# A decoder layer's state-space mixer: eight resident Toeplitz tiles, a re-ordered prologue and a token buffer with the chunk index innermost

## The reference

```
x = x + mixer(layernorm(x))       # diagonal state-space scan, projection 256 -> 256, its own residual
x = x + cross_attention(layernorm(x), ctx)     # 16 heads of 16, 64 keys
x = x + ffn(layernorm(x))         # 256 -> 2x1024 gated -> 1024 -> 1024 -> 256

mixer(u):  xn = layernorm(u) * gamma + beta
           h[t] = exp(-exp(log_A) dt) h[t-1] + (B dt) xn[t]       # 64 states per channel
           y[t] = sum_n C[n] h[t][n] + D xn[t]
           return u + y @ W_out.T + b_out
```

## Time and profile before

| | before |
|---|---|
| median of 3 runs | 929.63 us (928.91 to 930.36) |
| the profiled execution, its own time | 931.86 us |
| its span, first to last instruction | 929.9 us |
| PE / PEld busy | 865.2 us (93%) / 703.3 us (76%) |
| DVE / ACT / POOL busy | 524.3 (56%) / 483.3 (52%) / 183.7 us (20%) |
| granted TensorE clock, mean | 0.985 |
| code fetched by PE's queue (q8) | 24 packets, 0.39 MB |

### The profile page before, as it was taken

The page is one execution under the profiler, slowest core; times in us unless marked ns, Lnnn a source line. Parts: engine busy times, 40 slices in busy tenths (PEclk is TensorE's granted clock), DMA queues, the critical chain, the costliest instruction groups (busy, mean ns, idle before and its releaser), DMA issues.

```text
span 929.9 us, 15452 instructions
## 1 busy us (share of the span) xinstructions
PE 865.2 (93%) x5762; PEld 703.3 (76%) x5762; DVE 524.3 (56%) x943; ACT 483.3 (52%) x745; POOL 183.7 (20%) x201
## 2 busy tenths in 40 slices
PE   1168999899999999999999999999999999999998
PEld 0067867677887778777877787778777887788887
DVE  7996486465556455555655555464655456464422
ACT  2926543566347634754366536753576256734432
POOL 1567710500031002300130005000500040003000
PEclk9689999999999999999999999999999999999999
DMA  9962698500110002000200010001100110001000
GB/s 341 246 169 50 228 386 344 227 1 1 39 58 0 0 23 73 0 0 0 73 22 0 0 62 34 0 0 51 45 0 0 51 45 0 0 23 45 1 1 25
DMA packets 15641, 61.92 MB, mean 67 GB/s; under 512 B 2851, under 2 KB 4646, under 8 KB 14790
## 3 DMA queue, kind: packets, MB, share of 16 engines
q1 hardware_dynamic: 15574, 61.44, 19.2%
q0 software_dynamic: 32, 0.00, 0.0%
HBM read 49.76 MB, written 23.20 MB: 78 GB/s over the span
## 4 chain that ended last, share of the span: by engine, by line
PE 83%; DVE 9%; issue 5%; ACT 2%; DVEq 0%; POOL 0%; DMA 0%; SPq 0%; POOLq 0%
PE pair L1348 44%; PE pair L1335 9%; PE pair L1360 6%; PE pair L1374 4%; PE pair L1277 4%; PE pair L1288 3%; PE pair L1304 3%; PE pair L470 2%; PE pair L477 2%; PE pair L1297 1%; PE pair L1244 1%; PE pair L484 1%; PE pair L539 1%; DVE vbuf L1150 1%; DVE GG L337 1%
## 5 line engine op out<-in xcount | busy, mean ns | idle before, releaser
L952 ACT ACTIVATE vbuf<-pair,scl 128x512 f32<-128x512 f32 x128 | 87.7, 685 | 231.0 <-PE pair L1348 227.8
L1348 PE MATMUL pair<-h2hi,h_turned 128*128 128x512 f32 x512 | 202.7, 396 | 0.0
L1348 PE MATMUL pair<-h2lo,h_turned 128*128 128x512 f32 x512 | 199.5, 390 | 0.0
L1348 PE MATMUL pair<-h1hi,h_turned 128*128 128x512 f32 x384 | 153.4, 399 | 0.0
L1348 PE MATMUL pair<-h1lo,h_turned 128*128 128x512 f32 x384 | 150.1, 391 | 0.0
L1114 DVE TENSOR_TENSOR h1lo<-vbuf,h1hi 128x512 fp32r<-128x512 f32 x80 | 57.7, 722 | 119.5 <-ACT h1hi L953 118.7
L1348 PEld LDWEIGHTS pair<-h2hi,h_turned 128*128 128x128 f32 x512 | 96.1, 188 | 25.2 <-issue 5.9
L1348 PEld LDWEIGHTS pair<-h2lo,h_turned 128*128 128x128 f32 x512 | 96.2, 188 | 19.3
L1114 DVE TENSOR_TENSOR h2lo<-vbuf,h2hi 128x512 fp32r<-128x512 f32 x64 | 44.3, 692 | 107.0 <-ACT h2hi L953 106.7
L1335 PE MATMUL pair<-zThi,w_turned 128*128 128x512 f32 x224 | 91.7, 410 | 4.1 <-DVE vbuf L1150 4.1
L1348 PEld LDWEIGHTS pair<-h1hi,h_turned 128*128 128x128 f32 x384 | 72.1, 188 | 24.7 <-issue 10.5
(11 more groups left out here) (143 smaller groups left out, 1584.5 us busy)
## 6 DMA issues: line engine op xcount, KB each, us to landing
h_turned<-d_h SPq DMA_DIRECT2D x2, 4096.0 KB, 15.0
xres<-in_x SPq DMA_DIRECT2D x8, 512.0 KB, 7.4
tok<-in_xs SPq DMA_DIRECT2D x8, 512.0 KB, 12.2
EE<-alpha_rows SPq DMA_DIRECT2D x16, 256.0 KB, 11.0
ring<-kernel_rows SPq DMA_DIRECT2D x16, 256.0 KB, 4.2
xr<-x_rows SPq DMA_DIRECT2D x8, 512.0 KB, 3.5
out<-xr SPq DMA_DIRECT2D x16, 256.0 KB, 2.0
x_rows<-xres SPq DMA_DIRECT2D x7, 512.0 KB, 12.5
```

Source lines behind the costliest of these rows:

```text
L952: e.activation(vb[:, s % 2, :], h_ps[s % 4], ACT.Gelu, scale=sc)
L1348: ins = e.matmul(bank, w[:, k, m * P:(m + 1) * P], src[part][:, k, :], start=(k == 0 and part == 0), stop=(k == HC - 1 and part == 1))
```

## The change

- **Tiles.** TT has eight tiles instead of four; the four new ones lie where w1 and w2 are loaded later, the row sums `ksb` where w3 is. All sixteen `tt_load` DMAs are issued in the prologue, in turn with the remaining EE groups; bo, woT, xW, keys and scl come behind them. `sync_core` waits for `w_ps` before it loads w1 to w3.
- **POOL.** The D addition and the restoring of GG's column move from DVE to POOL. Masks 0 to 7 all run in `gpsimd_core`, not before `z_h` is 3 (gamma of the third quarter block), and all bias sums follow them.
- **Layout.** tok is [partition, batch, channel, chunk]. Moving operands of `state` and `within` are runs of 15 or 16 tokens; one column of `norms`, `norm_apply` and the tile that `y_turn` transposes are 64 bytes from element to element. x is loaded in 8 DMAs of 64 partitions x 8 KB instead of 8 of 128 x 4 KB.
- **Sharing.** ACT takes 16 columns of each 32, DVE 16 (12 before). ACT takes the statistics of tiles 8 to 15 (a Copy with its sum, then a Square with its sum, into PSUM scratch), DVE those of the other 24.
- **PE.** The row sums accumulate in one PSUM pair with a selecting column (`pick`), and five matmuls of 128x512 whose result nobody reads stand between `z_b` = 2 and the octet loop.
- **Order.** DVE: `norms(1)` goes behind `beta(1)`; its memsets go to its start.

```diff
-ACT_SHARE = 20
+ACT_SHARE = 16
+ACT_STATS = (8, 16)
+ROWS_AT = 3
...
-    tok = nc.alloc_sbuf_tensor_at("tok", [P, BC, P], F32, offset=t["zone_a"])
+    tok = nc.alloc_sbuf_tensor_at("tok", [P, BATCH, P, CH], F32, offset=t["zone_a"])
...
-        for g in range(8):
-            e.dma_start(tok[:, 8 * g:8 * g + 8, :], a["xs"][:, 8 * g:8 * g + 8, :]).then_inc(x_in[g], 16)
+        for b in range(BATCH):
+            for h in range(2):
+                here = slice(L * h, L * h + L)
+                e.dma_start(tok[:, b, here, :], a["xs"][:, b, here, :]).then_inc(x_in[b], 16)
...
-        e.dma_start(bo[:, :], a["ab"].partition_broadcast(P)).then_inc(wo_in, 16)
-        e.dma_start(woT[:, :, :], a["aW"]).then_inc(wo_in, 16)
-        for v in range(4):
-            for h in range(2):
-                u = 2 * v + h
-                e.wait_ge(k_ev, u + 1)
-                c = (1 - h) * (P * L) + v * 2048
-                e.dma_start(kr[0, c:c + 2048].rearrange("(q m) -> q m", q=4), ksb[0:P:32, u, :]).then_inc(kr_st, 16)
-        for n in ("xW", "keys", "scl"):
-            e.dma_start(t[n], a[n]).then_inc(k_in, 16)
+        for h in range(2):
+            e.wait_ge(k_ev, h + 1)
+            for v in range(4):
+                c = (P * (1 - h) + 32 * v) * PAD
+                e.dma_start(kr[0, c:c + 32 * PAD].rearrange("(q m) -> q m", q=4), ksb[v:P:32, h, :]).then_inc(kr_st, 16)
         e.wait_ge(kr_st, 128)
         e.wait_ge(kr_pad, 16)
         for g in range(4):
             tt_load(e, g)
-        for g in range(2, NGRP):
+            if g in (1, 2):
+                entries_load(e, g + 1)
+        for g in range(4, NGRP):
             entries_load(e, g)
+            if g == 6:
+                e.wait_ge(nat_v, 1)
+            tt_load(e, g)
+        e.dma_start(bo[:, :], a["ab"].partition_broadcast(P)).then_inc(wo_in, 16)
+        e.dma_start(woT[:, :, :], a["aW"]).then_inc(wo_in, 16)
+        for n in ("xW", "keys", "scl"):
+            e.dma_start(t[n], a[n]).then_inc(k_in, 16)
 
     def sync_core(e):
-        for g in range(4, NGRP):
-            e.wait_ge(w_ps, 2 * (g - 4) + 2)
-            tt_load(e, g)
...
+    def gpsimd_core(e):
+        e.wait_ge(z_h, 3)
+        for g in range(NGRP):
             mask(e, g)
...
+        for tile in range(TILES):
+            bias(e, tile)
...
+            for j in range(first, until):
+                e.activation(junk[j % 4], xres[:, j, :], ACT.Copy, accum_out=tsum[:, 0, j:j + 1]).then_inc(t_sum, 1)
...
+            for j in range(first, until):
+                e.activation(junk[j % 4], xres[:, j, :], ACT.Square, bias=tsum[:, 1, j:j + 1], scale=1.0 / 16, accum_out=mvn[:, j, 1:2]).then_inc(t_var, 1)
...
         gamma(0)
-        norms(1)
         beta(0)
         gamma(1)
         beta(1)
+        norms(1)
         gamma(2)
         beta(2)
...
+        e.wait_ge(z_b, 2)
+        for _ in range(5):
+            e.matmul(pair[3][:, 0:BLK], ident[:, :], GGf[:, 0:BLK], start=True, stop=True)
...
-                rhs = tok5[L * h:L * h + L, i, :, 0:CH - 1]
+                rhs = tok[L * h:L * h + L, :, i, 0:CH - 1]
...
-            ins = e.transpose(bank[:, c * P:(c + 1) * P], tok[:, 8 * i + c, :], rev[:, :])
+            ins = e.transpose(bank[:, c * P:(c + 1) * P], tok[:, i // 2, :, 8 * (i % 2) + c], rev[:, :])
```

More of the change, by code:

```diff
@@ L79, in mixer_parts @@
     rev = sb("rev", [P, P], "c")
-    ones = sb("ones", [P, 32], "c")
+    pick = sb("pick", [P, 35], "c")
     stn = sb("stn", [P, TILES, 6], "d")
@@ L113, in mixer_parts @@
     yps = [pair[k][:, 512 * h:512 * (h + 1)] for k in (2, 0) for h in range(2)]
-    kps = [[pair[k][:, 512 * h:512 * (h + 1)] for h in range(2)] for k in (2, 0)]
+    kps = [pair[2][:, 512 * h:512 * (h + 1)] for h in range(2)]
+    junk = [pair[0][:, DM * k:DM * (k + 1)] for k in range(4)]
     ident = t["ident"]
@@ L220, in gpsimd_prep @@
         e.memset(rev[:, :], 0.0).then_inc(const, 1)
-        e.memset(ones[:, :], 1.0).then_inc(const, 1)
+        e.memset(pick[:, :], 0.0).then_inc(const, 1)
         e.memset(mhalf[:, :], -0.5).then_inc(const, 1)
@@ L240, in gpsimd_prep @@
             e.tensor_tensor(rn[:, 0, here], sv[:, here], mhalf[:, 0:SB], ALU.pow).then_inc(powd, 1)
-        mask(e, 0)
-        e.wait_ge(t_mask, 2)
+        e.wait_ge(d_in, 32)
+        e.wait_ge(w_row, 2)
+        e.wait_ge(g_row, 7)
+        for row in (0, N):
+            v = GG[row:row + 1, :, L - 1]
+            e.tensor_tensor(v, v, edit[row:row + 1, 0, :], ALU.add).then_inc(d_add, 1)
+        e.wait_ge(d_add, 2)
+        power(0)
+        e.wait_ge(k_ps, 1)
+        e.wait_ge(powd, 1)
+        for row in (0, N):
+            e.tensor_copy(GG[row:row + 1, :, L - 1], edit[row:row + 1, 1, :]).then_inc(g_back, 1)
+        e.wait_ge(g_back, 2)
+        power(1)
         e.wait_ge(nat_v, 1)
+        e.wait_ge(powd, 2)
         e.tensor_tensor(rsm[:, :], svn[:, :], mhalf[:, :], ALU.pow).then_inc(natural, 1)
         e.wait_ge(natural, 1)
-        for g in range(1, 4):
+    def gpsimd_core(e):
+        e.wait_ge(z_h, 3)
+        for g in range(NGRP):
             mask(e, g)
-        e.wait_ge(t_mask, 8)
-    def gpsimd_core(e):
+        e.wait_ge(t_mask, 2 * NGRP)
         e.wait_ge(wo_in, 32)
-        done = 0
-        for g, until in ((4, 0), (5, 0), (6, 0), (7, 4), (None, TILES)):
-            for tile in range(done, until):
-                bias(e, tile)
-            done = until
-            if g is not None:
-                e.wait_ge(base_b, done)
-                mask(e, g)
-                e.wait_ge(t_mask, 2 * g + 2)
+        for tile in range(TILES):
+            bias(e, tile)
     def scalar(e):
@@ L292, in residual_base @@
             e.activation(xres[:, j, :], xres[:, j, :], ACT.Identity, bias=ngn[:, j:j + 1], scale=rsn[:, j:j + 1]).then_inc(base, 1)
-        for v in range(4):
-            row_evac(v)
-        e.wait_ge(const, 9)
+        for first in range(*ACT_STATS, 4):
+            tile_stats(first, first + 4)
+        e.wait_ge(const, 10)
         norm_apply(0)
-        entry_exp(0)
         norm_apply(1)
-        for g in range(1, 3):
+        for g in range(3):
             entry_exp(g)
@@ L321, in vector @@
     def vector(e):
+        for k in range(2):
+            e.memset(hps[k], 0.0).then_inc(h_zero, 1)
+        e.memset(dec[:, :, 0], 0.0).then_inc(dec0, 1)
         e.wait_ge(exps, 2)
@@ L330, in vector @@
         e.tensor_copy(GG[:, :, L - 1:L], wT.unsqueeze(2)).then_inc(g_row, 1)
-        for row in (0, N):
-            e.tensor_copy(edit[row:row + 1, 1, :], wT[row:row + 1, :]).then_inc(d_add, 1)
         def double(k):
@@ L476, in within @@
                 rows = slice(L * h, L * h + L)
-                ins = e.matmul(yps[o % 4][rows, c * BC:(c + 1) * BC], TT[o // 2 % 4][rows, (i % GRP) * L:(i % GRP + 1) * L], tok[rows, :, i], start=(c == 0), stop=False)
+                ins = e.matmul(yps[o % 4][rows, c * BC:(c + 1) * BC].rearrange("p (b c) -> p b c", b=BATCH), TT[o // 2 % 8][rows, (i % GRP) * PAD:(i % GRP) * PAD + L], tok[rows, :, i, :], start=(c == 0), stop=False)
             return ins
```

140 lines of the change are left out of this document (79 added, 61 removed).

## The result

The changed kernel takes **932.96 us** (median of 19 runs, 930.95 to 936.13) against 930.24 us of the kernel before on the same chip (19 runs, 928.91 to 932.65): ratio 1.0026, 95% interval 1.0018 to 1.0034, so 1.7 to 3.2 us slower. The forecast was 932.7 us and "slower". The profiled execution took 933.36 us, its span 931.6 us, 1.5 and 1.7 us more than the profiled one of before.

The account below looks back on a forecast made before the run. The loop was taken as fed by code packets, 3.8 us each, later behind data transfers. Start -1.0, clock -0.6, loads +3.0 and transposes +2.1 made +3.5, rounded to +3.1: 935.0 us profiled, 932.7 median, range 922.5 to 940.

Parts of the forecast that it names:

- Start of the loop: Ahead of octet loop: DVE work saved against dearer columns and waits (1.3, 0.8, 0.3); -1.0 us, bounds -5.2 and +5.5.
- Masks: In the loop: each tile group is loaded before it is needed, so PE does not wait; bias sums 0.
- Loads: In the loop: load backlog to 71.5 us gives three 3.0 us stops, removes 6.1 us; +3.0 us, bounds -6.1 and +4.4.
- the tokens come as 64-partition loads: Prologue loads: if partitions set the rate, 4.2 MB take 17.7 instead of 10.1 us, backlog ending near 75 us.
- The clock: First product group of the loop: five idle matmuls bring the granted clock to 1.00 beforehand; -0.6 us, bounds -1.5 and 0.
- Moving operands in runs: In the loop: cheaper `state` and `within` bring nothing while a packet needs 3.8 us; 0, bounds -2 and 0.
- my list: Signs expected in the changed profile, among them three "issue" stops of 2.5 to 3 us before 75 us, none over 0.5 after.
- Transposes: Mostly in the head: weight loads of lone elements cost PE more, a third of 6.3 us showing; +2.1 us, bounds 0 and 6.3.
- Rival (a): In the loop: code packets get through the backlog and stops vanish; -4.1 us, 925.5 us, down to 922; chance 0.30.
- Rival (c): ACT's statistics and the transposes are both dear: start +4, transposes +6.3, stops +3; 942 to 943 us; chance 0.10.
- Rival (d): In the loop: the tiles do not do what they are for; part of the main case, whose chance is 0.40.
- (b): It cancels: backlog over at 68 us (two stops and a part), transposes nearly free; within 1.9 us of now; chance 0.20.

Follow-up runs that it names:

- e1_paced: Changed kernel, but tile groups 4 to 7 (TT) are loaded one by one inside the octet loop again; 929.6 us, ratio 0.9994 to the kernel before.
- e7_shift: Changed kernel with 128 increments of an unused semaphore at the head of PE's stream; 948.18 us, ratio 1.0192 to the kernel before.
- e12_tokens_half: Changed kernel, but each token load goes into 64 partitions with rows of 8192 bytes instead of 128 with 4096; 939.75 us, ratio 1.01 to the kernel before.
- e4_flat_turn: Changed kernel, but the 64 transposes read contiguous elements, leaving out the right order of y; 931.91 us, ratio 1.0022 to the kernel before.
- e3_wide: Changed kernel, but entries and tiles come from distinct rows of x in DRAM, with wrong operands; 933.25 us, ratio 1.0028 to the kernel before.
- e5_pairs: Changed kernel, but entries and tiles come two groups a transfer, rows of 8192 bytes in 64 partitions; 934.5 us, ratio 1.0049 to the kernel before.

## Why the prediction came out as it did

The number is closer than its working. By parts, against the sum of +3.5 us before rounding; the profiled span showed +1.7, the medians +2.7:

1. **Start of the loop: forecast -1.0, measured -4.9 us**, just inside the bound of -5.2. Of the 3.9 us between, 0.7 are the norms: 32 columns took 9.85 us where 24 took 7.93 before, +1.9 and not +2.6 with the contention gone. 0.8 is the third `beta`, 1.22 instead of 2.04 us: the first select now begins at 45.12, beside it, and only DVE's next two pay 2.17. The other 2.4 us are the step that failed, the waits: I had summed 1.3 + 0.8 + 0.3 for them and, by subtraction, nothing net is left. ACT's statistics ended at 18.24 us (0.37 and 0.46 us a pass, 0.19 for each read of the accumulator), ahead of DVE's last doubling at 19.15, where I had 20.3. The estimate by a 591 ns pass was too dear. The timelines of DVE and of ACT in the changed kernel (start, us, engine, line, operation):

```profile
28.08 4.91 DVE L419 TENSOR_SCALAR tok<-tok,spread 128x128 f32<-128x128 f32 x16
...
45.04 1.22 DVE L433 TENSOR_TENSOR tok<-tok,bet 128x1024 f32<-128x1024 f32 x1
46.18 2.17 DVE L428 TENSOR_TENSOR tok<-tok,gam 128x1024 f32<-128x1024 f32 x1
...
17.65 0.46 ACT L310 ACTIVATE pair<-xres,tsum 128x256 f32<-128x256 f32 x1
18.05 0.19 ACT L310 ACTIVATION_READ_ACCUMULATOR pair<-xres,tsum 128x1 f32 x1
```

2. **Masks: forecast "PE does not wait", measured 1.95 us**, which takes back part of the start's gain. I had priced the later groups of tiles and not the first, though I had written that the masks start behind `gamma(2)`. Two selects of some 2.1 us from 45.12 end at 49.4, and the loop was ready at 47.5.

3. **Loads: forecast +3.0 us from three stops of 3.0; they are 3.17, 3.72 and 3.98**, +4.8 over what was removed. The mechanism is the one predicted, code packets that come late behind data transfers; e1_paced, e7_shift and e12_tokens_half bear it out. But one step that led to it was a misreading: "the tokens come as 64-partition loads". `here` in their load slices the channels, not the partitions, so "8 DMAs of 64 partitions x 8 KB" under "The change" is wrong too: they are 8 of 128 partitions x 4 KB, as before, and moved 415 GB/s, as before. My middle value of 71.5 us for the end of the backlog came near the measured end (share 0.70 in 66 to 76 us, 0.01 from 76) by luck. By my own terms slow tokens would have given 69 + 7.6 = 76.6 us, not 75. e12_tokens_half is the kernel that I had in mind, and it takes 6.8 us more. What kept the value near was that I gave this step only half of its weight.

4. **The clock: forecast -0.6 us by five idle matmuls.** It did rise ahead of the loop, and it fell again at 50.7 us, to 0.50 or 1.2 GHz, behind PE's wait for the first mask, and stayed low to the end of the row below; from 80 us on it was 1.00. What the idle matmuls gave is in no run by itself. Rows of the changed kernel, from the rise on:

```profile
43.90:50.70 6.80, 4.47 (x124) 2.87 (x125) 6.77 (x8) 1.21 (x2) 5.31 (x4) 1.00 1.04 228
50.70:67.80 17.10, 10.21 (x282) 9.84 (x278) 10.92 (x18) 2.23 (x3) 15.02 (x11) 0.50 1.03 228
```

Between deep stops PE goes on at 55.11, 63.78 and 72.2 us, 8.7 and 8.4 apart, of which it works 5.0 and 4.5 at the low clock. If the next packet is asked for where PE goes on, a fast clock would only lengthen the stop; no run here tried it, so what the low clock cost stays open.

5. **Moving operands in runs: 0, measured 0 net.** The tiles' product took 291 ns; now its mean is 287 in the ring and 234 in the other four tiles. The two differ by the clock, not by the tile: from 50.7 to 72 us, at the low clock, the ring's took 319 ns, and behind 80 us, at 1.00, 235. At 1.00 `state` fell likewise, from 272 to 218 ns, while `carried`, whose operands the change leaves alone, went only from 225 to 220. PE's execution fell by 5.1 us in all, in spite of the low clock. The stops behind 80 us are now 5.3 us in sum and up to 1.35 each, where they were 2.2 us before, and my list had said "none over 0.5". The list contradicted point 5: PE goes on at 89.91, 94.03, 97.98 and 101.65 us, 3.9 a packet, about the 3.8 of before. What is executed faster is waited for longer.

6. **Transposes: forecast +2.1, measured at most +0.1**, if nothing else behind the loop changed: that is all by which the rest of the span grew. The weight load grew from 140 to 194 ns, by 54 and not 132, and hardly any of it came to the path.

So -3.9 (start) + 1.95 (mask) + 2.2 (loop: 6.52 - 1.95 = 4.57 against 3.0 - 0.6) - 2.0 (transposes) = -1.8 us, which is 1.7 - 3.5. Each of these four errors is larger than the +1.7 us itself: the right sign and a near number came from errors that cancelled. Rival (a), the stops vanish, fell: three deep stops stand in the chain. With it falls, for this loop, the "mostly hidden" of the Trainium skill, "Runtime: NRT & Kernel Launch", "Instruction fetch mechanics". Rival (c) fell in both its halves. Rival (d), that the ring brings nothing, is what e1_paced shows. (b), within 1.9 us of the kernel before, was near and is touched by the interval; of its two conditions the nearly free transposes came, two stops and a part did not.

Left open is the spread between executions. In quiet stretches the profiled ones of e1_paced and e4_flat_turn need some 3.45 us a packet, those of the changed kernel, e3_wide and e5_pairs 3.7 to 3.9. Over six packets that is some 2 us, as much as the whole effect; I don't know what sets it. No version beat both kernels: e1_paced, the change without its early tile loads, ties with the kernel before.

## What to carry over

Where a stream of short matmuls lives on code packets, time gained ahead of it or inside it is only worth something if the packets come sooner: look at the places of the "issue" stops, count instructions between them, and see what the data transfers do there. Prefetching everything early is not free; it puts a backlog in front of the code. Before costing a transfer, read which axis of the pattern is the partition and what the first dimension of both patterns is: 64 partitions nearly halved the rate here (415 to 230 GB/s), and a leading 2 left two engines of sixteen.

## What the hardware showed that I had not expected

- Rows of 8192 bytes into 64 partitions moved no faster than rows of 4096 (217 against 228 GB/s), and the stops of PE were deeper (3.95 to 4.62 us against 3.17 to 3.98).
- A product of 64x64 whose 64 moving elements lie in runs of 16 took 235 ns, against 291 ns with 512 bytes from one to the next, both at a granted clock of 1.00.
- A transfer with a source pattern that begins with 2 ran at a DMA share of 0.13 and 52 GB/s, and cost the kernel 109 us.
- A semaphore increment in PE's stream took some 0.12 us (128 of them moved PE's first matmul from 5.12 to 20.57 us), against 10 to 13 ns for one of the loop's instructions (256 of them in 2.7 to 3.4 us between quiet stops).
- The granted clock fell to 0.50 inside the loop, beside a PE that was busy 10.21 of 17.10 us; before, it stayed at 0.97 on average over the loop.
